# Interleaving the next group's LayerNorm and quantization with the scan of the current group, in a bidirectional state-space layer with a quantized gate

## The chip, the cores and the metric

The kernel runs on all 8 cores of one Trainium2 chip. Each core computes one sequence of the batch by itself; nothing is exchanged. The metric is the device time of the slowest core, in microseconds (us). It is given as the median of several executions. Engines are named as in the profile: PE is TensorE's matmul, PEld its weight load, DVE VectorE, ACT ScalarE, POOL GpSimd, SP SyncE. A "q" behind a name (POOLq) is the queue from which that engine issues DMAs.

## The reference, cut to what matters

Each core has `u` of 4096 x 1024. The layer is a residual around a product of a recurrent branch pair and a gate:

```
xn = layernorm(u)                                  # 1024 wide
zxbcdt = xn @ in_proj_w.T                          # z 2048, x 2048, B 64, C 64, dt 16
branch(zxbcdt, conv_w, dt_bias, A_log, D):
    dt = softplus(dt + dt_bias); A = -exp(A_log)
    x, B, C = split(silu(causal_conv4(xBC)))       # 16 heads of 128
    h_t = h_{t-1} * exp(dt_t*A) + dt_t * x_t B_t'  # state 64 per head
    y_t = h_t C_t + D*x_t
    yz = y * silu(z)
    return yz * rsqrt(mean(yz^2) + eps) * norm_w
s = (branch forward + branch on the reversed sequence, reversed back) @ out_proj_w.T
g = silu(mx_quantize(xn) @ mx_quantize(W).T + bias)   # blocks of 32, 6-bit grid
out = u + s * g
```

## The kernel before

The sequence is cut into 16 groups of `G` = 256 positions, each of two chunks of `Q` = 128. `pass_A` goes over the groups from the last to the first and runs the backward branch up to its scan; it stores the in-projection and the branch's output to HBM. `pass_B` goes forward over the groups: it loads both, computes the gate's two products (`z` and the quantized FFN product), the forward convolution and scan, then gating, norm, out-projection and residual.

Each engine has its own instruction stream, in program order, written out by one Python program that is run once per engine. Order between engines is kept by counting semaphores: `tp` counts PE, `ts` ACT, `tv` DVE, and `qs`, `qu`, `qx`, `qd`, `qo` and others count DMAs of one purpose. In `p.op`, a wait given as a pair such as `("tv", tvm)` is for a marked count; a wait given as a string such as `"ts"` is for the count of everything issued on that semaphore up to this place in the program. Waits are instructions of their own in the stream of the waiting engine, so whatever stands behind a waiting instruction waits too. Each DMA issue also waits for the DMA before it on the same semaphore.

A group of `pass_A` runs: in-projection (L914 to L924), convolution (`conv_dir`, DVE), transposes of its result to `Xtm` and `Btm` (SP), `dt_pipeline` (short operations of DVE and ACT, ending in six small DMAs `s_scr`, `sflat`, `b3c` on ACT's queue), then `pro` for the next group (L974), then `scan_chunk` for both chunks. A group of `pass_B` has the matmuls for `z` and the FFN first and four additions and two Silu for `gff` (L1262, L1272) behind `dt_pipeline`; then `pro` and the two `scan_chunk` again.

`pro` does, for each of the two 128-row tiles of the next group: load `u2` on GpSimd's queue, `ln_tile` (statistics on DVE, Ln and Exp on ACT at L361 and L365, the result `xn2` on DVE), a transposing DMA to `xnT`, and in `pass_B` also `quantize_tile` (two halves of some fifteen DVE operations, L1004 to L1086, ending in `xd2`) and a transposing DMA to `xdT`. Both tiles use the one buffer `u2`, so the second load waits for the first tile's DVE operations. The load's waits are `"tv"` and `"qo"`.

`scan_chunk` has a first part for each half `hq` of the heads: PE forms the decay sums in PSUM, ACT takes their Exp twice (`gq` at L687, `mtq` at L704; for `hq` 1 both lie in the tile `ur`), and DVE makes from them `bwq`, `diagq`, `gcq` and the final `mtq` (L709 to L746, the mark `opv` behind them). The second part, again for each half, is 32 small matmuls in two blocks of 16 (L777 to L787) with ACT's copies to `hT` (L790) and `convX` (L797). For `hq` 1 DVE makes a new `gcq` (L757) first. The first matmul of a chunk and the decay sums wait on `"ts"`, the Exp at L704 on `"tv"`:

```
            mm(ps[:, 3072:3072 + 128], v["convBC"][0:64, 0, csl],
               v["convBC"][0:64, 1, csl], True, True,
               wait=["ts", ("tv", tvm), "qd", "qy"])
...
                p.op("scalar",
                     lambda e, mtq_h=mtq_h, dsl=dsl: e.activation(
                         mtq_h, ps[:, dsl], AF.Exp),
                     wait=[("tp", t2v), "tv"], inc="ts")
```

Of the kernel before, what the change touches and what calls it, by code (L numbers as in the profile page):

```python
# [20 lines left out]
G = 256  # L21
NG = L // G
# [65 lines left out]
def make_program(debug=0):  # L88
# [133 lines left out]
    def prog(nc, p):  # L222
        shared = {}
# [3 lines left out]
        dr = state["dr"]  # L227
        sb = state["sb"]
# [13 lines left out]
        def ld(dst, src, wait=(), inc="qc", q="scalar"):  # L242
            p.op(q, lambda e: e.dma_start(out=dst, in_=src),
                 wait=wait, inc=inc, dma=True)
# [403 lines left out]
                         in_=dr["s_scr"][:, 3 + j_, :]),  # L648
                     inc="qd", dma=True)

        def scan_chunk(dirn, c, hTa, hTb, q_rot, tvm):
            anchor = (Q - 1) if dirn == "fw" else 0
            csl = slice(c * Q, (c + 1) * Q)
            v = sb
# [8 lines left out]
               wait=["ts", ("tv", tvm), "qd", "qy"])  # L663
            p.op("scalar",
                 lambda e: e.copy(v["cbt"][:], ps[:, 3072:3072 + 128]),
                 wait=["tp"], inc="ts")
            cbv = p.mark("ts")
            ph = []
            for hq in range(2):
# [11 lines left out]
                   wait=["qd", "ts", ("tv", tvm)])  # L681
# [7 lines left out]
                     wait=[("tp", t1v), "ts", ("tv", tvm)], inc="ts")  # L689
                gv = p.mark("ts")  # L690
                for nn in range(2):
# [4 lines left out]
                       wait=[("ts", gv)] if nn == 0 else ())  # L696
# [20 lines left out]
                     wait=[("ts", mtv), ("ts", cbv), "tv", "qo"],  # L717
                     inc="tv")
# [8 lines left out]
                     wait=["tv"], inc="tv")  # L727
                if hq == 0:
# [7 lines left out]
                         wait=["tv"], inc="tv")  # L736
# [7 lines left out]
                     wait=["tv"], inc="tv")  # L744
# [4 lines left out]
                     wait=["tv"], inc="tv")  # L749
                opv = p.mark("tv")  # L750
                ph.append((h0, pd, mtq_h, gq_h, bwq_h, diagq_h, opv))
            for hq in range(2):
                h0, pd, mtq_h, gq_h, bwq_h, diagq_h, opv = ph[hq]
                if hq == 1:
# [8 lines left out]
                         wait=[("tp", ymv0), "tv"], inc="tv")  # L763
                    opv = p.mark("tv")
                for half4 in range(2):
                    sev = p.mark("ts")
                    for hh4 in range(4):
# [7 lines left out]
                        elif hh4 == 0:  # L775
# [3 lines left out]
                           wait=w0)  # L779
# [14 lines left out]
                         wait=[("tp", smv)], inc="ts")  # L794
# [6 lines left out]
                     wait=[("tp", ymv)], inc="ts")  # L801
# [14 lines left out]
        def pass_A():  # L816
# [16 lines left out]
            for i in range(8):  # L833
                ld(sb["um"][:], dr["fwt"][i * 128:(i + 1) * 128, :],
                   wait=["tv"], inc="qw")
# [4 lines left out]
                qv = p.mark("tv")  # L840
                p.op("scalar",
                     lambda e, i=i: e.dma_start(
                         out=dr["wbfF"][i * 128:(i + 1) * 128, :],
                         in_=sb["xd2"][:, 0, :]),
                     wait=[("tv", qv)], inc="qw", dma=True)
                mk_st = p.mark("qw")
            shared["qfv"] = p.mark("qw")
            q_rot = [0, 0]
            rot = {"n": 0, "mk": [0, 0]}

            def pro(t0):
                for s_ in range(2):
                    ld(sb["u2"][:],
                       dr["u"][t0 + s_ * 128:t0 + (s_ + 1) * 128, :],
                       wait=["tv", "qo"], inc="qu", q="gpsimd")
                    ln_tile(s_, False)
                    xnv = p.mark("tv")
                    tpv = p.mark("tp")
                    p.op("sync",
                         lambda e, s_=s_, xnv=xnv, tpv=tpv: e.dma_start(  # L860
                             out=sb["xnT"][:, :, s_ * 128:(s_ + 1) * 128],
                             in_=sb["xn2"][:, s_, :].rearrange(
                                 "p (k f) -> p k f", k=8),
                             transpose=True),
                         wait=[("tv", xnv), ("tp", tpv), ("qs", wTv)],
                         inc="qs", dma=True)
                return p.mark("qs")

            prev = {"tv": p.mark("tv"), "ts": p.mark("ts"),
                    "tp": p.mark("tp")}  # L870
            xv = pro((NG - 1) * G)
            for gi in range(NG - 1, -1, -1):
                if gi == 2:
                    bbo = sb["warena"][:, 32768:40960].rearrange(
                        "p (t c) -> p t c", t=4)
                    for c0 in range(0, 8, 4):
# [18 lines left out]
                        out=sb["nwtile"][:],  # L895
                        in_=dr["normw"].rearrange("(k f) -> f k", f=128),
# [6 lines left out]
                                               transpose=True),  # L903
                         wait=[("qw", None)], inc="qs", dma=True)
# [23 lines left out]
                def halo_bw():  # L928
# [13 lines left out]
                         out=dr["sp_x"][gi],  # L942
# [31 lines left out]
                if gi > 0:  # L974
                    xv = pro((gi - 1) * G)
# [119 lines left out]
        def pass_B():  # L1095
# [26 lines left out]
            for half in range(2):  # L1122
# [23 lines left out]
            yzn_ap = sb["Xtm"][:].rearrange("p m q -> p (m q)").rearrange(  # L1146
                "p (i t) -> p i t", i=NH)

            def pro(t0):
                for s_ in range(2):  # L1150
                    ld(sb["u2"][:],
                       dr["u"][t0 + s_ * 128:t0 + (s_ + 1) * 128, :],
                       wait=["tv", "qo"], inc="qu", q="gpsimd")
                    ln_tile(s_, True)
                    xnv = p.mark("tv")
                    tpv = p.mark("tp")
                    p.op("sync",
                         lambda e, s_=s_, xnv=xnv, tpv=tpv: e.dma_start(
                             out=sb["xnT"][:, :, s_ * 128:(s_ + 1) * 128],
                             in_=sb["xn2"][:, s_, :].rearrange(  # L1160
                                 "p (k f) -> p k f", k=8),
                             transpose=True),
                         wait=[("tv", xnv), ("tp", tpv), ("qs", wdv)],
                         inc="qs", dma=True)
                    quantize_tile(sb["xd2"][:, s_, :], rst_is_one=False)
                    qv = p.mark("tv")
                    p.op("sync",
                         lambda e, s_=s_, qv=qv: e.dma_start(
                             out=sb["xdT"][:, :, s_ * 128:(s_ + 1) * 128],
                             in_=sb["xd2"][:, s_, :].rearrange(  # L1170
                                 "p (k f) -> p k f", k=8),
                             transpose=True),
                         wait=[("tv", qv)], inc="qs", dma=True)
                return p.mark("qs")

            prev = {"tv": p.mark("tv"), "ts": p.mark("ts"),
                    "tp": p.mark("tp")}
# [1 line left out]
            for gi in range(NG):  # L1179
# [95 lines left out]
                         wait=[("tv", gfv), "ts"], inc="ts")  # L1275
                ggv = p.mark("ts")
                tvm = p.mark("tv")
                if gi < NG - 1:
                    xv = pro(t0 + G)
                for c in range(CPG):  # L1280
                    p.op("tensor", lambda e: e.nop(),
                         wait=[("qs", trv), ("tv", tvm), "ts"])
                    scan_chunk("fw", c, sb["hT0"][:], sb["hT0"][:], q_rot,
                               tvm)
                yfv = p.mark("ts")
                opvs = [None, None]
                urvs = [None, None]
# [207 lines left out]
```

How the kernel before makes its waits and increments, by code:

```python
    def op(self, eng_name, fn, wait=(), inc=None, dma=False):  # L66
        if self.eng_name == eng_name:
            for w in wait:
                if isinstance(w, str):
                    s, v = w, self.cnt[w]
                else:
                    s, v = w
                    if v is None:
                        v = self.cnt[s]
                self.eng.wait_ge(self.h[s], v)
            if dma and inc is not None:
                self.eng.wait_ge(self.h[inc], self.cnt[inc])
            instr = fn(self.eng)
            if inc is not None:
                instr.then_inc(self.h[inc], 16 if dma else 1)
        if inc is not None:
            self.cnt[inc] += 16 if dma else 1
```

## Time and profile before

| | us |
|---|---|
| median of 3 runs (lowest, highest) | 7017.65 (7011.57, 7019.2) |
| the profiled execution, whole | 7007.59 |
| its span, core 0 (all cores 6983.4 to 7006.0) | 7006.0 |
| PE busy | 2635.8 (38%) |
| DVE busy | 2894.5 (41%) |
| ACT busy | 1314.3 (19%) |
| mean granted TensorE clock | 0.591 of 2.4 GHz |
| pass A's groups, from about 290 to 2950; pass B's from about 3020 to the end | |

Busy times are of one core. A row of the order of time gives the start, the duration, the engine, the line and the operation with its tiles, and in brackets how long the engine had been idle and what released it. Where a wait was for several semaphores, the one that came last by the profile is named. Merged rows carry a count (x2). All matmuls have the line of the helper `mm` (L239) and all loads by `ld` that of L243, so tiles tell them apart.

### The profile page before, as it was taken

How to read it: one execution, taken by the hardware profiler on the slowest of the kernel's cores; microseconds unless marked ns; L12 is line 12 of the kernel's file. 1: busy time of each engine (PE TensorE's matmuls, PEld its weight loads, DVE VectorE, ACT ScalarE, POOL GpSimd, SP SyncE). 2: the span in 40 equal slices, each digit the busy share in tenths (PEclk: the TensorE clock that was granted, in tenths of full speed). 3: DMA queues.
4: the chain of work that ended last, by engine and by line, in shares of the span. 5: the costliest groups of instructions: out<-in, count | busy, mean ns of one | idle time of the engine just before them, and what ended most of it. 6: DMA issues, size and time to landing. Idle time of an engine off the chain costs nothing.

```text
span 7006.0 us, 47131 instructions; the slowest of 8 cores (6983.4 to 7006.0 us)
## 1 busy us (share of the span) xinstructions
PE 2635.8 (38%) x12296; PEld 1268.2 (18%) x12296; DVE 2894.5 (41%) x5730; ACT 1314.3 (19%) x1939; POOL 125.4 (2%) x234
## 2 busy tenths in 40 slices
PE   0133444444433234315225334433522533443354
PEld 0011122222211112102112112111211211221121
DVE  2533333333443133353454354354345335435433
ACT  0021222222212112112111212211211221211112
POOL 0000000000000000000000000000000000000000
PEclk9955555555555555556566556556656655655665
DMA  4111110111111321121010011011101001110100
GB/s 91 40 33 34 35 29 29 29 29 35 35 29 35 88 58 35 44 60 32 19 42 26 22 41 34 26 27 37 31 19 42 26 22 41 35 33 20 41 28 19
DMA packets 364339, 250.45 MB, mean 36 GB/s; under 512 B 319456, under 2 KB 321761, under 8 KB 355890
## 3 DMA queue, kind: packets, MB, share of 16 engines
q0 software_dynamic: 30448, 132.95, 6.1%
q1 hardware_dynamic: 297216, 74.76, 5.4%
q10 hardware_dynamic: 36418, 39.72, 1.7%
q8 instruction: 110, 1.80, 0.1%
q14 instruction: 147, 1.20, 0.1%
HBM read 117.33 MB, written 68.19 MB: 26 GB/s over the span
## 4 chain that ended last, share of the span: by engine, by line
DVE 31%; PE 29%; DMA 14%; ACT 14%; issue 10%; DVEq 1%; ACTq 1%; POOLq 0%; POOL 0%; SPq 0%
PE ps L239 29%; DVE qv L424 6%; DVE convX L432 3%; DMA u<-u 2%; ACT convX L797 2%; DMA sflat<-s_scr 2%; DVE convX L404 2%; ACT convX L509 2%; DMA b3c<-s_scr 2%; DMA stgX<-sp_x 1%; ACT Xtm L1305 1%; DVE convX L410 1%; DVEq L75 1%; ACT hT L790 1%; DMA ybw<-sp_y 1%
## 5 line engine op out<-in xcount | busy, mean ns | idle before, releaser
L239 PE MATMUL ps<-convBC 64*128 64x128 bf16 x64 | 16.8, 262 | 2553.0 <-DVE um L371 1335.9
L239 PE MATMUL ps<-xnT,warena 128*128 128x256 bf16 (+2 forms) x4480 | 595.1, 294 | 457.6 <-DMA xnT<-xn 194.7
L239 PEld LDWEIGHTS ps<-xnT,warena 128*128 128x128 bf16 (+2 forms) x4480 | 441.6, 106 | 614.0 <-issue 524.2
L424 DVE TENSOR_TENSOR qv<-stgX,cwX 128x1012 bf16<-128x1012 bf16 x384 | 465.8, 1213 | 40.7 <-DVE convX L432 0.9
L239 PEld LDWEIGHTS ps<-convBC 64*128 64x128 bf16 x64 | 6.4, 100 | 2569.6 <-issue 2569.6
L239 PE MATMUL ps<-sflat,ones 3*64 3x512 bf16 (+1 forms) x512 | 282.7, 603 | 461.3 <-ACT mtq L704 244.6
L709 DVE TENSOR_TENSOR bwq<-Btm,mtq 128x512 bf16<-128x512 bf16 x64 | 44.3, 692 | 807.2 <-ACT mtq L704 807.2
L239 PE MATMUL ps<-warena,Xtm 128*128 128x512 bf16 x1024 | 293.5, 457 | 179.9 <-DVE u L1390 102.6
L790 ACT CAST hT<-ps 64x512 bf16<-64x512 f32 x256 | 148.2, 579 | 1019.7 <-PE ps L239 1019.7
L239 PE MATMUL ps<-gcq,hT 64*128 64x128 bf16 x1024 | 292.3, 285 | 0.0
L404 DVE TENSOR_SCALAR convX<-stgX,cwX,cbX 128x253 bf16<-128x253 bf16 x512 | 175.9, 343 | 273.5 <-ACT stgX L909 208.7
L432 DVE TENSOR_TENSOR convX<-convX,qv 128x1012 bf16<-128x1012 bf16 x384 | 264.6, 689 | 40.7 <-DVE qv L424 0.9
L509 ACT ACTIVATE convX<-convX 128x4096 bf16<-128x4096 bf16 x32 | 115.7, 3616 | 603.4 <-DVE convBC L503 603.3
L361 ACT ACTIVATE mv<-mv,epsb 128x1 f32<-128x1 f32 x64 | 18.8, 294 | 1022.5 <-DVE mv L357 762.8
L239 PE MATMUL ps<-ur,Xtm 128*128 128x128 bf16 x512 | 145.3, 284 | 162.7 <-ACT convX L797 110.2
L239 PE MATMUL ps<-mtq,Xtm 128*128 128x128 bf16 x512 | 145.0, 283 | 136.9 <-ACT ur L704 84.8
L757 DVE TENSOR_TENSOR gcq<-ur,convBC 64x1024 bf16<-64x1024 bf16 x64 | 43.7, 683 | 333.8 <-PE ps L239 333.8
L239 PEld LDWEIGHTS ps<-warena,Xtm 128*128 128x128 bf16 x1024 | 113.7, 113 | 352.4 <-issue 277.6
L353 DVE BATCH_NORM_STATS2 bns<-u 128x6 f32<-128x512 f32 x64 | 44.4, 694 | 318.3 <-DMA u<-u 318.3
L239 PE MATMUL ps<-Xtm,ones128b 128*1 128x128 bf16 x1024 | 95.5, 267 | 203.8 <-ACT Xtm L1305 203.8
L1338 DVE CAST rbc<-ps 128x256 bf16<-128x256 f32 x32 | 13.6, 424 | 383.8 <-PE ps L239 383.8
L239 PEld LDWEIGHTS ps<-sflat,ones 3*64 3x64 bf16 (+1 forms) x512 | 48.0, 116 | 666.8 <-issue 666.8
(164 smaller groups left out, 4845.3 us busy)
## 6 DMA issues: line engine op xcount, KB each, us to landing
u<-u POOLq DMA_DIRECT2D x64, 512.0 KB, 4.0
sp_x<-stgX POOLq DMA_DIRECT2D x16, 1024.0 KB, 4.2
sp_y<-convX POOLq DMA_DIRECT2D x16, 1024.0 KB, 4.8
stgX<-sp_x POOLq DMA_DIRECT2D x16, 1024.0 KB, 6.4
ybw<-sp_y POOLq DMA_DIRECT2D x16, 1024.0 KB, 5.0
ur<-u POOLq DMA_DIRECT2D x32, 512.0 KB, 4.0
out<-ostg ACTq DMA_DIRECT2D x32, 256.0 KB, 2.0
out<-u ACTq DMA_DIRECT2D x32, 256.0 KB, 2.5
```

Of the source, the lines that this page charges most:

```text
L75: self.eng.wait_ge(self.h[s], v)
L239: lambda e: e.matmul(out_ap, lhsT, rhs, start=start, stop=stop),
L353: p.op("vector", lambda e: e.bn_stats(sb["bns"][:, 0:6], uap[:, 0:512]), wait=["qu", "tv"], inc="tv")
L404: lambda e, i=i: e.tensor_scalar(cvX[:, i, osl0], stX[:, i, isl0], sb["cwX"][:, i, 0:1], sb["cbX"][:, i:i + 1], op0=ALU.mult, op1=ALU.add),
L410: lambda e, i=i: e.tensor_scalar(cvX[:, i, esl0], sb["haloX"][:, i, hsl0], sb["cwX"][:, i, 0:1], sb["cbX"][:, i:i + 1], op0=ALU.mult, op1= ...
L424: e.tensor_tensor(scr3, stX[:, t4, isl], sb["cwX"][:, t4, tap:tap + 1].broadcast_to([128, 4, n_main]), op=ALU.mult),
L432: e.tensor_tensor(cvX[:, t4, osl], cvX[:, t4, osl], scr3, op=ALU.add),
L509: lambda e: e.activation(cvX[:].rearrange("p i t -> p (i t)"), cvX[:].rearrange("p i t -> p (i t)"), AF.Silu),
L709: lambda e, bwq_h=bwq_h, mtq_h=mtq_h: e.tensor_tensor(bwq_h.rearrange("p (h n) -> p h n", h=8), v["Btm"][:, c, :].unsqueeze(1).broadcast_t ...
L790: lambda e, h0=h0, half4=half4: e.copy(hTb[:, (h0 + half4 * 4) * 128: (h0 + half4 * 4 + 4) * 128], ps[0:64, 3584:3584 + 512]),
L797: lambda e, h0=h0, pd=pd, csl=csl: e.copy(sb["ystg"][:, h0:h0 + 8, csl], ps[:, pd:pd + 1024].rearrange("p (h t) -> p h t", h=8)),
L1305: lambda e, buf=buf, tsl=tsl: e.activation(yzn_ap[:, :, tsl], sb[buf][:, :, tsl], AF.Square),
```

## The change

`pro` is cut into four pieces, `pa` and `pb` for each tile, in both passes. `pa` is the load and `ln_tile`; `pb` is the transposing DMA and, in `pass_B`, `quantize_tile` with its transposing DMA. `scan_chunk` gets an argument `fill_fn`, which is called right behind the Exp at L704, before DVE's `bwq`, and issues the next piece. The two chunks with two halves each take all four pieces in order: load and norm of tile 0, transpose (and quantization) of tile 0, the same two for tile 1. The operations themselves, and what each waits for by name, are unchanged; the counts that a string wait and a mark stand for are those at the new places. The first group of each pass still has its prologue in one block, and the last has none.

```diff
-        def scan_chunk(dirn, c, hTa, hTb, q_rot, tvm):
+        def scan_chunk(dirn, c, hTa, hTb, q_rot, tvm,
+                       fill_fn=None):
...
                 mtv = p.mark("ts")
+                if fill_fn is not None:
+                    fill_fn()
                 p.op("vector",
...
+            def pro_pieces(t0):
+                pieces = []
+                for s_ in range(2):
+                    def pa(s_=s_):
+                        ld(sb["u2"][:],
+                           dr["u"][t0 + s_ * 128:t0 + (s_ + 1) * 128, :],
+                           wait=["tv", "qo"], inc="qu", q="gpsimd")
+                        ln_tile(s_, True)
+
+                    def pb(s_=s_):
+                        xnv = p.mark("tv")
+                        tpv = p.mark("tp")
+                        p.op("sync",
+                             lambda e, s_=s_, xnv=xnv, tpv=tpv: e.dma_start(
+                                 out=sb["xnT"][:, :,
+                                              s_ * 128:(s_ + 1) * 128],
+                                 in_=sb["xn2"][:, s_, :].rearrange(
+                                     "p (k f) -> p k f", k=8),
+                                 transpose=True),
+                             wait=[("tv", xnv), ("tp", tpv), ("qs", wdv)],
+                             inc="qs", dma=True)
+                        quantize_tile(sb["xd2"][:, s_, :], rst_is_one=False)
+                        qv = p.mark("tv")
...
+                        shared["xvB"] = p.mark("qs")
+                    pieces.append(pa)
+                    pieces.append(pb)
+                return pieces
...
-                if gi < NG - 1:
-                    xv = pro(t0 + G)
+                fills = pro_pieces(t0 + G) if gi < NG - 1 else []
+
+                def ff(fills=fills):
+                    if fills:
+                        fills.pop(0)()
                 for c in range(CPG):
                     p.op("tensor", lambda e: e.nop(),
                          wait=[("qs", trv), ("tv", tvm), "ts"])
                     scan_chunk("fw", c, sb["hT0"][:], sb["hT0"][:], q_rot,
-                               tvm)
+                               tvm, fill_fn=ff)
+                while fills:
+                    fills.pop(0)()
+                if gi < NG - 1:
+                    xv = shared["xvB"]
```

`pass_A` is changed alike, with `ln_tile(s_, False)`, no quantization and `shared["xvA"]`. `pro` itself now calls the four pieces one after the other.

## Rows read from the trace of the kernel before

**Rows 1.** The page's first line.

```profile
span 7006.0 us, 47131 instructions; the slowest of 8 cores (6983.4 to 7006.0 us)
```

**Rows 2.** Waits of PE: who waited <- for whom, us in total, times, longest.

```profile
PE ps L239 <- DVE um L371: 1335.9, 15, 91.4
PE ps L239 <- ACT mv L365: 1013.9, 15, 68.3
```

**Rows 3.** Order of time, ACT, pass A, first and fifteenth group.

```profile
383.17 0.29 ACT L361 ACTIVATE mv<-mv,epsb 128x1 f32<-128x1 f32 x1 [17.52 <-DMA b3c<-s_scr]
383.55 0.20 ACT L365 ACTIVATE mv<-mv 128x1 f32<-128x1 f32 x1
...
393.67 0.27 ACT L665 CAST cbt<-ps 128x128 bf16<-128x128 f32 x1 [1.00 <-PE ps L239]
...
2707.82 0.29 ACT L361 ACTIVATE mv<-mv,epsb 128x1 f32<-128x1 f32 x1 [17.29 <-DMA b3c<-s_scr]
...
2718.58 0.27 ACT L665 CAST cbt<-ps 128x128 bf16<-128x128 f32 x1 [1.03 <-PE ps L239]
```

**Rows 4.** The same, group 0 of pass A, with no prologue behind it.

```profile
2873.45 3.49 ACTq L646 DMA_DIRECT2D b3c<-s_scr  x3
2878.77 0.27 ACT L665 CAST cbt<-ps 128x128 bf16<-128x128 f32 x1 [28.68 <-PE ps L239]
```

**Rows 5.** The same, pass B, first and fifteenth group.

```profile
3136.28 2.20 ACT L1272 ACTIVATE gff<-gff 128x1024 bf16<-128x1024 bf16 x2
...
3246.41 1.00 ACT L797 CAST convX<-ps 128x1024 bf16<-128x1024 f32 x1
...
6625.01 2.20 ACT L1272 ACTIVATE gff<-gff 128x1024 bf16<-128x1024 bf16 x2
...
6735.23 1.00 ACT L797 CAST convX<-ps 128x1024 bf16<-128x1024 f32 x1
```

**Rows 6.** The same, last group of pass B, with no prologue behind it.

```profile
6874.43 2.20 ACT L1272 ACTIVATE gff<-gff 128x1024 bf16<-128x1024 bf16 x2
...
6879.45 1.28 ACT L687 ACT_TABLE_LOAD   x1 [1.47 <-PE ps L239]
...
6948.00 1.00 ACT L797 CAST convX<-ps 128x1024 bf16<-128x1024 f32 x1
...
6956.02 0.36 ACT L1318 ACTIVATE rrow<-ps,epsb 1x128 bf16<-1x128 f32 x1 [2.16 <-PE ps L239]
```

**Rows 7.** The same, group 7 of pass B.

```profile
4928.93 1.02 ACT L704 ACTIVATE mtq<-ps 128x1024 bf16<-128x1024 f32 x1 [13.63 <-DVE xd L1086]
```

**Rows 8.** Order of time, DVE, group 7 of pass B.

```profile
4884.92 0.75 DVE L376 TENSOR_SCALAR xn<-um,mv 128x1024 bf16<-128x1024 f32 x1 [5.24 <-ACT mv L365]
4885.77 0.69 DVE L1004 TENSOR_REDUCE qsc<-um 128x16 f32<-128x512 f32 x1
...
4901.32 0.69 DVE L1086 TENSOR_TENSOR xd<-qv,qsc 128x512 bf16<-128x512 f32 x1 [0.17 <-DVE qsc L1082]
...
4930.26 0.69 DVE L709 TENSOR_TENSOR bwq<-Btm,mtq 128x512 bf16<-128x512 bf16 x1 [1.43 <-ACT mtq L704]
...
4933.43 0.69 DVE L746 TENSOR_TENSOR mtq<-mtq,ddiag 128x1024 bf16<-128x1024 bf16 x1
...
4945.66 0.68 DVE L757 TENSOR_TENSOR gcq<-ur,convBC 64x1024 bf16<-64x1024 bf16 x1 [5.25 <-PE ps L239]
```

**Rows 9.** DMA issues: tiles, queue, count, KB each, median us to landing.

```profile
u<-u POOLq DMA_DIRECT2D x64, 512.0 KB, 4.0
...
xnT<-xn SPq DMA_TRANSPOSE x64, 2.7
```

**Rows 10.** Order of time, PE, group 7 of pass B, first chunk's outputs.

```profile
4937.18 0.26 PE L239 MATMUL ps<-mtq,Xtm 128*128 128x128 bf16 x1 [1.32 <-ACT ur L704]
...
4947.21 0.27 PE L239 MATMUL ps<-ur,Xtm 128*128 128x128 bf16 x1 [1.72 <-ACT convX L797]
```

**Rows 11.** Stages: busy us and instructions by engine, clock, DMA share, GB/s.

```profile
4957.00:4993.00 36.00, 23.84 (x81) 8.99 (x81) 7.12 (x11) 8.58 (x12) 0.00 (x0) 0.50 0.00 1
```

More of the change, by code:

```diff
@@ L849, in pass_A @@
             rot = {"n": 0, "mk": [0, 0]}
-            def pro(t0):
[L852 to L867, printed above, removed]
+            def pro_pieces(t0):
[5 more added lines that the diff above has]
+                           wait=["tv", "qo"], inc="qu", q="gpsimd")
+                        ln_tile(s_, False)
+                    def pb(s_=s_):
[8 more added lines that the diff above has]
+                                 transpose=True),
+                             wait=[("tv", xnv), ("tp", tpv), ("qs", wTv)],
+                             inc="qs", dma=True)
+                        shared["xvA"] = p.mark("qs")
+                    pieces.append(pa)
+                    pieces.append(pb)
+                return pieces
+            def pro(t0):
+                for f in pro_pieces(t0):
+                    f()
+                return shared["xvA"]
             prev = {"tv": p.mark("tv"), "ts": p.mark("ts"),
@@ L973, in pass_A @@
                 tvm = p.mark("tv")
-                if gi > 0:
-                    xv = pro((gi - 1) * G)
+                fills = pro_pieces((gi - 1) * G) if gi > 0 else []
+                def ff(fills=fills):
+                    if fills:
+                        fills.pop(0)()
                 for c in range(CPG - 1, -1, -1):
@@ L1147, in pass_B @@
                 "p (i t) -> p i t", i=NH)
-            def pro(t0):
[L1150 to L1174, printed above, removed]
@@ new lines, in pro_pieces, with pa, pb @@
+            def pro_pieces(t0):
+                pieces = []
+                for s_ in range(2):
+                    def pa(s_=s_):
+                        ld(sb["u2"][:],
+                           dr["u"][t0 + s_ * 128:t0 + (s_ + 1) * 128, :],
+                           wait=["tv", "qo"], inc="qu", q="gpsimd")
+                        ln_tile(s_, True)
+                    def pb(s_=s_):
+                        xnv = p.mark("tv")
+                        tpv = p.mark("tp")
+                        p.op("sync",
+                             lambda e, s_=s_, xnv=xnv, tpv=tpv: e.dma_start(
+                                 out=sb["xnT"][:, :,
+                                              s_ * 128:(s_ + 1) * 128],
+                                 in_=sb["xn2"][:, s_, :].rearrange(
+                                     "p (k f) -> p k f", k=8),
+                                 transpose=True),
+                             wait=[("tv", xnv), ("tp", tpv), ("qs", wdv)],
+                             inc="qs", dma=True)
+                        quantize_tile(sb["xd2"][:, s_, :], rst_is_one=False)
+                        qv = p.mark("tv")
+                        p.op("sync",
+                             lambda e, s_=s_, qv=qv: e.dma_start(
+                                 out=sb["xdT"][:, :,
+                                              s_ * 128:(s_ + 1) * 128],
+                                 in_=sb["xd2"][:, s_, :].rearrange(
+                                     "p (k f) -> p k f", k=8),
+                                 transpose=True),
+                             wait=[("tv", qv)], inc="qs", dma=True)
+                        shared["xvB"] = p.mark("qs")
+                    pieces.append(pa)
+                    pieces.append(pb)
+                return pieces
@@ L1176, in pass_B @@
+            def pro(t0):
+                for f in pro_pieces(t0):
+                    f()
+                return shared["xvB"]
             prev = {"tv": p.mark("tv"), "ts": p.mark("ts"),
@@ L1283, in pass_B @@
                     scan_chunk("fw", c, sb["hT0"][:], sb["hT0"][:], q_rot,
-                               tvm)
+                               tvm, fill_fn=ff)
+                while fills:
+                    fills.pop(0)()
+                if gi < NG - 1:
+                    xv = shared["xvB"]
                 yfv = p.mark("ts")
```

5 lines of the change are left out of this document (added).

## The prediction

> **What bounds the kernel now.** Three views were read in this order. First the list of what TensorE (PE) waited for. Its two longest lines are waits in front of the scan, 1335.9 us in 15 groups of pass B, put down to the `um` operation, and 1013.9 us in 15 groups of pass A, put down to the Exp of `ln_tile` [rows 2]. Both belong to the prologue `pro` of the next group. So the question is what lies at the end of these waits. No engine is full; the kernel is one chain of PE, VectorE (DVE), ScalarE (ACT) and DMAs in which each stage waits for the one before.
>
> Then the order of time on ACT around the scan of pass A. After the last `b3c` DMA, ACT goes straight on to the Ln of the first tile, and the scan's first copy `cbt` comes 10.50 us after that Ln in the first group and 10.76 in the fifteenth (393.67 - 383.17, 2718.58 - 2707.82; the mean of the 15 is 10.67) [rows 3]. Group 0 has no prologue behind it. There `cbt` comes 2878.77 - 2876.94 = 1.83 us after the third `b3c` issue has ended [rows 4]. What fills the difference is the second tile: its load waits for the first tile's last DVE operation, because both use `u2`, and only when it has landed and has been normalised is the ACT count reached on which `scan_chunk`'s first matmul waits (`"ts"`, the count at that place of the program).
>
> Last, the same for pass B. From the end S of the second Silu at L1272 to the end of the scan's last copy it takes 3247.41 - 3138.48 = 108.93 us in the first group and 6736.23 - 6627.21 = 109.02 in the fifteenth, mean 108.9 [rows 5]. In the last group, which has no prologue, it takes 6949.00 - 6876.63 = 72.37 us [rows 6]. So the prologue costs 36.5 us a group here. It is on the path because the Exp at L704 waits for everything on DVE, both `quantize_tile` calls included: in group 7 it starts at 4928.93 after a 13.63 us wait for `xd` [rows 7].
>
> **What the change does, by parts.** The same instructions are issued, in four pieces per group instead of one block. A piece follows the Exp at L704 of each half `hq` of each chunk. Call the end of the hq 0 Exp M.
>
> *The front of the scan.* No prologue operation stands ahead of the first matmul any more. In pass A the gain is 10.67 - 1.83 = 8.8 us a group (third `b3c` DMA to first matmul as in group 0). In pass B S to the end becomes the 72.37 us of the last group plus what the pieces add inside the scan.
>
> *Piece 1 and piece 3 (load, `ln_tile`) at hq 0.* ACT does Ln and Exp behind the L704 Exp: 0.08 + 0.38 + 0.20 = 0.66 us [rows 3]. PE's matmuls for hq 1 wait on the ACT count, so they move by 0.7. That is on the path, twice a group: 1.4 us. The statistics of the first tile wait for nothing new (load released by the end of `dt_pipeline` or the `gff` adds, as before). On DVE `xn` starts about 0.9 after M and has a slot of 0.85 (4885.77 - 4884.92), then the five operations of hq 0 take 3.86 (4934.12 - 4930.26) [rows 8]: done at M + 5.6. In the scan as it is they end at M + 4.2 (M = 4929.95). The hq 1 Exp, which waits for them, starts at about M + 6.1 without the 0.7 (PE's outputs follow it at 4937.18 = M + 7.2, and it lasts 1.02 [rows 7, 10]) and at M + 6.75 with it, so this delay is covered with 1.1 us to spare. If that cover were gone it would cost the excess, tenths per chunk.
>
> *The second load.* It is queued on GpSimd behind nothing of the scan but the DVE count of the chunk before. In pass A this is about M + 16.4, as in the row of `gcq` (4945.66, 15.7 after M) [rows 8] plus 0.7. A load lands in a median of 4.0 us [rows 9], the two statistics and the aggregate take under 2.5, and the next hq 0 Exp ends 36 us after M. So some 12 us are spare (two equal chunks share about 71 of the 72.37 us, 35.4 each). Behind this load on GpSimd's queue stand only the `sp_y` store (pass A) and the `ur` load (pass B), both after the scan. The 4 to 6 us of this load and its statistics, which stood on the path, vanish into the first chunk.
>
> *Pieces 2 and 4 (transpose; in pass B also `quantize_tile`) at hq 1.* In pass A only a transpose on SyncE's queue. It now waits for matmuls of hq 1, lands in 2.7 us [rows 9], and the second one is out some 17 us before the scan ends. Nobody needs it before the next in-projection: nothing. What is queued behind it on SyncE is the next group's `Xtm` transpose, far later.
> In pass B one quantization takes 16.24 us of DVE (4885.77 to 4902.01 over two halves) [rows 8], ahead of hq 1's DVE work. It starts at M + 5.7 and ends at M + 21.95. It waits for no transpose: `xnT` is issued near M + 6.6 and lands before the first `xd` write near M + 13. Then four operations at a spacing of 0.79 (3.1), `gcq` (0.8) and 0.3 to PE: the hq 1 outputs start at M + 26.2. Without the pieces they start at 4947.21 - 4929.95 = M + 17.3 [rows 7, 10]. PE's hq 0 outputs and ACT's copies run meanwhile and are what hides the rest. This is 8.9 us a chunk, 17.8 a group; it holds the 0.7 of piece 1. The quantized tile's transpose, of the same size as `xnT`'s, ends inside the scan. The load of the second tile is released at M + 25.9, lands by M + 32 (I allow 6 us, half as much again as the median), and is normalised by M + 35, while the next M is 35.4 + 8.9 = 44.3 away: 9 us spare.
>
> *The activation table.* The load of 1.28 us in front of the Ln after Silu moves to the scan's first Exp, as in the last group (6879.45) [rows 6]. It is in the 72.37. The number of loads stays.
>
> **The sum.** Pass B: 108.9 - (72.4 + 17.8) = 18.7 us a group, times 15 = 280. Pass A: 8.8 - 1.4 = 7.4, times 15 = 111. Together 391. The profiled execution took 7007.59 (span 7006.0 [rows 1]); 7007.6 - 391 = 6617. The median of the runs shown lies 10 us, 0.14%, above the profiled one, so the forecast for the median is 6625, 5.6% less.
> Bounds of what the trace doesn't show, the DVE work inside the scan: below, it can't cost less than nothing, which would give 7007.6 - 15 x 36.5 - 15 x 8.8 = 6328, but DVE has only the gaps of each chunk, and the instruction order puts 16 us into one of them; above, that none of the quantization overlaps (first rival). I take the value from the order of instructions, which is nearest to the rows.
> TensorE's clock gives and takes nothing here: in the scan it is granted 0.50, 1.2 GHz, as it is [rows 11], so the new pauses cannot lower it, and the stages behind the scan start from the same state.
>
> **Rivals.**
> (a) *The quantization is not hidden by the hq 0 outputs.* If the first output matmuls also waited for piece 2, they would start after M + 22 and hq 1's about 10.0 later (4947.21 - 4937.18) [rows 10], at M + 32.3: 6.1 us more a chunk, 183 in all, 6810. For it: many waits here take "the count so far" of an engine. Against it: the mark `opv` that these matmuls wait for is taken before the piece is issued.
> (b) *Ln between two Exps costs table loads.* Two loads per `ln_tile`, four a group, 30 groups, by the row of 1.28 us [rows 6]: 154 us, 6780. Against it: in the last group the table was loaded for an Exp, and a Ln at 6956.02 followed with no load between [rows 6]. The Trainium skill ("ScalarE: Activation LUTs", Table sets: the hidden batching unit) says the same, that one set holds both exp and ln. Its section What ACT_TABLE_LOAD costs gives about 2.66 us for a switch, drain included; by that this rival would be 30 x 4 x 2.66 = 319 us, 6945. Where page and row differ I go by the row.
> (c) *Slower: the second tile's load comes late.* It is now between the chunks, on DVE and ACT ahead of the scan's own work of the second chunk, so a late load stops everything. It has 9 to 12 us to spare, and a group saves 7.4 or 18.7, so it would decide the sign only if the load took some 22 to 34 us instead of 4 to 6. At 40 us each, pass A would lose about 15 a group and pass B 6: 7330. Against it: the load is alone in its queue, and its wait ends in chunk one.
> (d) *No change*: the waits only move. This needs DVE's whole prologue to stay on the path in both passes; the second load alone contradicts it.
>
> **How the numbers follow.** Forecast 0.86, with a range of its own from 6585 to 6665 (1.3 us a group either way). Rival (a) 0.05, (b) 0.03, (c) 0.02, (d) 0.01, and 0.03 for a mixture that keeps part of the gain. The range 6565 to 6685 leaves out the rivals and a little of the forecast's tails. Faster by over 0.2% (about what a measurement of this kernel can tell from no change) is everything but (c) and (d) and a part of the mixture: 0.96; within it 0.015; slower 0.025.
>
> **What would show it.** PE's two long waits give way to one for `b3c` (pass A) and one for the second `gff` Silu (pass B). In pass A `cbt` stands about 2 us behind the last `b3c` issue, and the scan is 1.4 us longer than in group 0. In pass B S to the end of the scan is 90 us, with a PE gap of about 9 us ahead of each hq 1 output block, put down to `gcq` or DVE. The first load of a group stays where it is, the second lands inside the first chunk's last third (pass A) or between the chunks (pass B). 15 table loads move from L361 to L687. The prediction is wrong if the hq 0 outputs wait for `xd`, if `bns` waits for `u` in the second chunk with PE idle, or if DVE's operations beside PE and DMA traffic take longer than these rows.

## The result and the profile after

The changed kernel takes 6632.96 us in the median of 8 runs (6627.3 to 6635.53), against 7013.83 us (7008.1 to 7022.59) for the kernel before in the same comparison: a ratio of 0.9454, 95% interval 0.9444 to 0.9464, or 381 us less. A second comparison on another chip gave 0.9468 (0.9452 to 0.9484). The forecast was 6625 us, with a range from 6565 to 6685.

The page of the profile after, its span and the busy times:

```profile
span 6627.3 us, 47131 instructions; the slowest of 8 cores (6602.0 to 6627.3 us)
...
PE 2633.1 (40%) x12296; PEld 1267.4 (19%) x12296; DVE 2893.6 (44%) x5730; ACT 1315.4 (20%) x1939; POOL 125.2 (2%) x234
```

All busy times are those of before to within 3 us. The same work stands closer together.

What PE waited for, in the changed kernel (engine, releaser, us in total, times, longest):

```profile
PE ps L239 <- ACT gff L1309: 981.2, 16, 63.8
PE ps L239 <- DMA b3c<-s_scr: 955.3, 16, 71.5
PE ps L239 <- DVE gcq L760: 307.5, 30, 10.5
...
PE ps L239 <- ACT mv L365: 127.4, 60, 2.4
```

The `um` line of [rows 2] is gone, and the line of `mv` has fallen from 1013.9 us to 127.4. In their place stand the waits that the prediction named: the second `gff` Silu in pass B, 981.2 us in 16 groups where the `um` line had 1335.9 in 15, and the last `b3c` DMA in pass A. These are now the length of the stages ahead of the scan. Inside the scan two lines are to be read. The 30 waits for `gcq`, 307.5 us or 10.25 each, are new. The 60 for the Exp of `ln_tile` (`mv`) last 2.1 us each; they stand where PE waited for the Exp at L704 before, for 1.4 us wherever DVE didn't hold that Exp up.

ACT in order of time, pass A, the first and the fifteenth group, which answers to [rows 3]:

```profile
376.50 3.69 ACTq L646 DMA_DIRECT2D b3c<-s_scr  x3
381.94 0.27 ACT L666 CAST cbt<-ps 128x128 bf16<-128x128 f32 x1 [19.53 <-PE ps L239]
...
389.68 0.29 ACT L361 ACTIVATE mv<-mv,epsb 128x1 f32<-128x1 f32 x1
390.06 0.20 ACT L365 ACTIVATE mv<-mv 128x1 f32<-128x1 f32 x1
...
2597.61 3.46 ACTq L646 DMA_DIRECT2D b3c<-s_scr  x3
2602.88 0.27 ACT L666 CAST cbt<-ps 128x128 bf16<-128x128 f32 x1 [18.75 <-PE ps L239]
```

The third `b3c` issue ends at 380.19, and `cbt` comes 1.75 us later, as in group 0 [rows 4]. Ln and Exp now stand in the scan, right behind the chunk's first Exp at L705 (L704 before). Over the 15 groups the distance from the last `b3c` issue to `cbt` fell from 10.8 to 1.9 us and the scan grew from 70.06 to 71.36.

The same for pass B, which answers to [rows 5]:

```profile
3026.60 2.21 ACT L1309 ACTIVATE gff<-gff 128x1024 bf16<-128x1024 bf16 x2
...
3118.43 1.01 ACT L800 CAST convX<-ps 128x1024 bf16<-128x1024 f32 x1
...
6265.79 2.21 ACT L1309 ACTIVATE gff<-gff 128x1024 bf16<-128x1024 bf16 x2
...
6357.58 1.01 ACT L800 CAST convX<-ps 128x1024 bf16<-128x1024 f32 x1
```

From the end of the second Silu to the end of the scan it takes 3119.44 - 3028.81 = 90.63 us in the first group and 6358.59 - 6268.00 = 90.59 in the fifteenth, in the mean of the 15 90.79. It was 108.92. The last group, which has no pieces, has 72.2 as before.

One group of pass B (the ninth), its first chunk on ACT:

```profile
4887.09 1.28 ACT L688 ACT_TABLE_LOAD   x1 [1.47 <-PE ps L239]
4888.38 1.02 ACT L688 ACTIVATE gq<-ps 64x1024 bf16<-64x1024 f32 x1
4892.97 1.02 ACT L705 ACTIVATE mtq<-ps 128x1024 bf16<-128x1024 f32 x1 [3.57 <-PE ps L239]
4894.08 0.30 ACT L361 ACTIVATE mv<-mv,epsb 128x1 f32<-128x1 f32 x1
```

The table load has moved from the Ln to the first Exp, and the Ln behind the Exp at L705 needs none. M, the end of that Exp, is 4893.99. On DVE (`qsc` at L1027 is the first operation of a quantization, `xd` its last):

```profile
4894.92 0.75 DVE L376 TENSOR_SCALAR xn<-um,mv 128x1024 bf16<-128x1024 f32 x1 [13.67 <-ACT mv L365]
4895.84 0.69 DVE L712 TENSOR_TENSOR bwq<-Btm,mtq 128x512 bf16<-128x512 bf16 x1 [0.17 <-DVE xn L376]
...
4899.01 0.69 DVE L749 TENSOR_TENSOR mtq<-mtq,ddiag 128x1024 bf16<-128x1024 bf16 x1
4899.81 0.69 DVE L1027 TENSOR_REDUCE qsc<-um 128x16 f32<-128x512 f32 x1
...
4903.51 0.29 DVE L1079 TENSOR_SCALAR qm<-qau 128x512 bf16<-128x512 bf16 x1
4904.26 0.29 DVE L1083 TENSOR_SCALAR qm<-qau 128x512 bf16<-128x512 bf16 x1 [0.46 <-DVE qm L1079]
...
4915.70 0.69 DVE L1109 TENSOR_TENSOR xd<-qv,qsc 128x512 bf16<-128x512 f32 x1 [0.17 <-DVE qsc L1105]
4916.57 0.69 DVE L712 TENSOR_TENSOR ostg<-Btm,ur 128x512 bf16<-128x512 bf16 x1 [0.17 <-DVE xd L1109]
...
4919.74 0.68 DVE L760 TENSOR_TENSOR gcq<-ur,convBC 64x1024 bf16<-64x1024 bf16 x1
4925.00 0.69 DVE L353 BATCH_NORM_STATS2 bns<-u 128x6 f32<-128x512 f32 x1 [4.58 <-DMA u<-u]
...
4926.91 0.75 DVE L371 TENSOR_SCALAR um<-u,mv 128x1024 f32<-128x1024 f32 x1
```

And on PE, the first output block of hq 0 and those of hq 1 of both chunks:

```profile
4901.91 0.26 PE L239 MATMUL ps<-mtq,Xtm 128*128 128x128 bf16 x1 [1.32 <-ACT ur L705]
...
4920.68 0.26 PE L239 MATMUL ps<-ur,Xtm 128*128 128x128 bf16 x1 [10.49 <-DVE gcq L760]
...
4965.23 0.26 PE L239 MATMUL ps<-ur,Xtm 128*128 128x128 bf16 x1 [10.13 <-DVE gcq L760]
```

The queue of DVE is to be read against M. `xn` starts at M + 0.9, `bwq` at M + 1.9, and the hq 0 work ends at M + 5.7. The quantization fills M + 5.8 to M + 22.4, `gcq` of hq 1 ends at M + 26.4, and PE starts the hq 1 outputs at M + 26.7 after 10.49 us of waiting. The hq 0 outputs started at M + 7.9, straight behind ACT's Exp and not behind `xd`: some 7 us of the quantization are hidden there. The second tile is loaded and `um` written by M + 33.7; the next Exp ends 44.9 after M.

The second chunk as a stage (busy us of PE, PEld, DVE, ACT, POOL, the granted clock, DMA share, GB/s), beside [rows 11]:

```profile
4931.00:4976.00 45.00, 23.79 (x81) 8.97 (x81) 21.43 (x42) 8.98 (x13) 0.00 (x0) 0.50 0.05 12
```

It takes 9 us more than before for the same PE work, DVE is busy 21.43 us instead of 7.12, and the clock stays at 0.50.

### The profile page after: what moved, and what is told of

Its sections match the earlier page's. It is cut to its first block, busy times and chain, and to the rows that moved or that the text cites. A ratio compares the mean times of both kernels' runs of the same rounds, so it can differ in the third digit from the quotient of the medians.

```text
span 6627.3 us, 47131 instructions; the slowest of 8 cores (6602.0 to 6627.3 us)
## 1 busy us (share of the span) xinstructions
PE 2633.1 (40%) x12296; PEld 1267.4 (19%) x12296; DVE 2893.6 (44%) x5730; ACT 1315.4 (20%) x1939; POOL 125.2 (2%) x234
## 4 chain that ended last, share of the span: by engine, by line
DVE 35%; PE 26%; DMA 14%; ACT 13%; issue 10%; DVEq 1%; ACTq 1%; POOLq 0%; POOL 0%; SPq 0%
PE ps L239 26%; DVE qv L424 7%; DVE convX L432 3%; DMA b3c<-s_scr 2%; DMA sflat<-s_scr 2%; DVE convX L404 2%; ACT convX L509 2%; ACT convX L800 2%; DVEq L75 1%; ACT Xtm L1349 1%; DMA stgX<-sp_x 1%; DVE convX L410 1%; DMA ybw<-sp_y 1%; DVE qv L468 1%; ACT mtq L705 1%
## 5 line engine op out<-in xcount | busy, mean ns | idle before, releaser
L239 PE MATMUL ps<-convBC 64*128 64x128 bf16 x64 | 16.8, 262 | 2008.3 <-ACT gff L1309 981.2
L239 PE MATMUL ps<-sflat,ones 3*64 3x512 bf16 (+1 forms) x512 | 282.9, 603 | 368.9 <-ACT mv L365 127.4
L239 PE MATMUL ps<-ur,Xtm 128*128 128x128 bf16 x512 | 144.0, 281 | 418.9 <-DVE gcq L760 307.5
L382 DVE TENSOR_SCALAR xn<-u,mv 128x1024 bf16<-128x1024 f32 x32 | 26.0, 812 | 419.9 <-ACT mv L365 419.9
L239 PE MATMUL ps<-mtq,Xtm 128*128 128x128 bf16 x512 | 144.0, 281 | 137.3 <-ACT ur L705 83.8
L376 DVE TENSOR_SCALAR xn<-um,mv 128x1024 bf16<-128x1024 f32 x32 | 24.1, 753 | 393.8 <-ACT mv L365 393.5
L239 PE MATMUL ps<-Xtm,bwq 128*64 128x128 bf16 x512 | 160.3, 313 | 0.0
L239 PE MATMUL ps<-Xtm,ostg 128*64 128x128 bf16 x512 | 160.3, 313 | 0.0
```

The costliest lines, as they stand in the source:

```text
L239: lambda e: e.matmul(out_ap, lhsT, rhs, start=start, stop=stop),
```

## The experiments

All ratios are to the kernel before, run beside it on the same chip. Three chips were used, and on them that kernel had medians of 7022.6, 7020.5 and 7017.3 us. Expectations are on a scale on which it has 7014 and the change 6633, so differences to the kernel before are compared, not times. Each such difference is known to about 10 us. Where a time per group is given, it is the mean of the 15 groups with a prologue in that run's trace. Line numbers shift by a few from one kernel to the next.

### Each pass alone

The pieces in pass A only, and in pass B only:

```diff
-                fills = pro_pieces(t0 + G) if gi < NG - 1 else []
+                fills = []
+                if gi < NG - 1:
+                    pro(t0 + G)
```

```diff
-                fills = pro_pieces((gi - 1) * G) if gi > 0 else []
+                fills = []
+                if gi > 0:
+                    pro((gi - 1) * G)
```

> The pieces in pass A alone; pass B keeps its prologue in one block. Theory (each group of pass A loses the 9.0 us in front of its scan and pays 1.3 us inside it, 15 groups): 115 us in the groups, of which the trace of the change kept 112, so 7014 - 113 = 6901 us. Rival (the two passes help each other, or part of the 381 us comes from somewhere else than the 30 prologues): this run and its counterpart do not add up to 381 us, by more than 10.

> The pieces in pass B alone. Theory (108.9 us from the second gff Silu to the end of the scan become 90.9, 15 groups): 7014 - 268 = 6746 us. Rival as for the counterpart: the two gains do not add up to 381 us.

Measured: pass A alone 6917.28 us, ratio 0.9849 (0.9834 to 0.9863), 105 us less. Pass B alone 6757.08 us, 0.9621 (0.9607 to 0.9636), 266 us less. Together 371, against 381 and 374 for the whole change in its two comparisons: the two gains add up to within what can be told. The gain comes from the 30 prologues, with no sign of another source. Pass A gave 8 us less than expected, which is within what a difference is known to. In its trace the distance and the scan changed as in the whole change (1.9 and 71.3 us), but its period per group fell by 7.2 us and not by 7.7, since the six small DMAs of `dt_pipeline` took 10.1 us a group there against 9.7 before. This is not shown to come from the change: with the pieces in pass B only, whose pass A is that of before, they took 10.3.

### The quantization in halves, and behind `gcq`

The first half of the columns stays where the change has the whole, and the second half is a third piece, `pc`, behind the hq 1 `gcq`. In pass A the third piece is empty.

```diff
-                        quantize_tile(sb["xd2"][:, s_, :], rst_is_one=False)
+                        quantize_tile(sb["xd2"][:, s_, :], rst_is_one=False,
+                                      halves=(0,))
+
+                    def pc(s_=s_):
+                        quantize_tile(sb["xd2"][:, s_, :], rst_is_one=False,
+                                      halves=(1,))
...
```

and behind the hq 1 `gcq` in `scan_chunk`:

```diff
                         wait=[("tp", ymv0), "tv"], inc="tv")
                     opv = p.mark("tv")
+                    if fill_fn is not None:
+                        fill_fn()
```

> The change, with each quantization cut in two: the first half of the columns stays between the hq 0 and hq 1 work of DVE, the second half goes behind the hq 1 gcq. Theory (what is left on the path in pass B is the part of a piece that is longer than the time that PE needs for the hq 0 outputs; half a quantization, 8.2 us, fits): hq 1 outputs start at M + 18 instead of M + 26.5 in each chunk, 8.4 us x 2 x 15 = 252 us less, 6381 us. Rival (any DVE work there delays the chunk by its length, and the second half delays the next chunk or the gating by its own): the sum of DVE work is the same, so 6633 us again, within 30.

Measured: 6395.5 us, ratio 0.9105 (0.909 to 0.9121), 627 us less than before and 246 less than the change. PE in a group of pass B, first outputs of hq 0 and hq 1:

```profile
4778.11 0.27 PE L239 MATMUL ps<-mtq,Xtm 128*128 128x128 bf16 x1 [1.32 <-ACT ur L705]
...
4788.74 0.27 PE L239 MATMUL ps<-ur,Xtm 128*128 128x128 bf16 x1 [2.36 <-DVE gcq L760]
```

DVE beside it (end of the first half, `gcq`, end of the second half):

```profile
4783.76 0.69 DVE L1113 TENSOR_TENSOR xd<-qv,qsc 128x512 bf16<-128x512 f32 x1 [0.17 <-DVE qsc L1109]
...
4787.80 0.68 DVE L760 TENSOR_TENSOR gcq<-ur,convBC 64x1024 bf16<-64x1024 bf16 x1
...
4795.95 0.69 DVE L1113 TENSOR_TENSOR xd<-qv,qsc 128x512 bf16<-128x512 f32 x1 [0.17 <-DVE qsc L1109]
```

M is 4770.18 here. The hq 1 outputs start at M + 18.6, after 2.36 us of waiting, and the second half ends at M + 26.5, before the next chunk needs DVE. The distance from the second Silu to the scan's end is 74.3 us, against 90.8. The same DVE operations in another order cost 16.5 us a group less. The rival, that the sum of DVE work decides, has fallen.

Then the whole quantization behind `gcq`: piece `pc` with both halves, none at hq 1.

> The change, with each whole quantization behind the hq 1 gcq of its chunk instead of between the hq 0 and hq 1 work of DVE. Theory: the hq 1 outputs no longer wait (8.9 us less a chunk), but in the first chunk the load of the second tile is released 7 us later than now and its statistics come about 4 us after the Exp that they follow, and in the second chunk DVE ends 5 us after the scan, which the gating waits for: 18 - 4 - 5.5 = 8 to 9 us a group less, 6633 - 130 = 6500 us, between 6480 and 6530. Rival (where the quantization stands does not matter as long as it is inside the scan): 6633 us, within 20.

Measured: 6547.09 us, ratio 0.9319 (0.9304 to 0.9335), 473 us less than before and 92 less than the change. The direction is the theory's, the size fell short of the least that was expected by about 10 us. DVE in a group (statistics of the second tile, last quantization of the second tile, first operation of the gating):

```profile
4898.28 0.69 DVE L353 BATCH_NORM_STATS2 bns<-u 128x6 f32<-128x512 f32 x1 [5.63 <-DMA u<-u]
...
4933.23 0.69 DVE L1113 TENSOR_TENSOR xd<-qv,qsc 128x512 bf16<-128x512 f32 x1 [0.17 <-DVE qsc L1109]
4934.02 1.23 DVE L1344 TENSOR_TENSOR convX<-convX,siluz 128x2048 bf16<-128x2048 bf16 x1
```

The two costs are there: the statistics come at 4898.28 with DVE idle for 5.63 us before, so the second chunk starts late, and the gating starts 0.1 us behind the last `xd`. The scan's last copy ended about 6 us earlier. From the Silu to the end of the scan the groups take 78.5 us, 12.3 less than in the change. The gating begins 5.8 us behind the scan in the mean where it began 0.2 behind it in the change, so 6.7 us a group are left, times 15 = 100; measured were 92. Of the three terms expected, the 18 us were the one that was off: the hq 1 outputs start 8.5 us earlier in each chunk, 17.0 in all, since the 0.7 us of Ln and Exp stay on the path. The late statistics cost 4.6 us where 4 were expected, and the gating 5.6 where 5.5 were.

### The quantization at hq 0

```diff
                 mtv = p.mark("ts")
-                if fill_fn is not None:
+                if fill_fn is not None and hq == 0:
+                    fill_fn()
                     fill_fn()
```

> The change, with transpose and quantization issued with the load and norm of their tile, at hq 0, ahead of DVE's hq 0 work: nothing is left for PE to do meanwhile but the decay sums of hq 1. Theory (7 us of each quantization are hidden by the hq 0 outputs and no more): hq 1 outputs at M + 33.5 instead of M + 26.5, 7 us x 2 x 15 = 210 us more, 6843 us. In pass A only the transpose moves: nothing. Rival (the quantization is not hidden by the hq 0 outputs at all, as one of the rivals of the prediction has it): no change against 6633 us.

Measured: 6855.73 us, ratio 0.9762 (0.9748 to 0.9777), 165 us less than before and 216 more than the change. Now PE waits ahead of the hq 0 outputs:

```profile
PE ps L239 <- ACT ur L705: 551.0, 64, 17.1
```

In the change this line had 83.8 us in 63 times. The Exp of hq 1 waits for all of DVE's hq 0 work, and the hq 0 outputs wait for that Exp, so with the quantization ahead of it PE has nothing to do. This measures what the hq 0 outputs hide in the change: 216 / 30 = 7.2 us a chunk.

### Load and norm ahead of the second Exp

The place of pieces 1 and 3 is moved ahead of the Exp at L705; pieces 2 and 4 stay.

```diff
                 t2v = p.mark("tp")
+                if fill_fn is not None and hq == 0:
+                    fill_fn()
                 p.op("scalar",
...
                 mtv = p.mark("ts")
-                if fill_fn is not None:
+                if fill_fn is not None and hq == 1:
                     fill_fn()
```

> The change, with load and norm (pieces 1 and 3) issued ahead of the second Exp of hq 0 instead of behind it; the quantization stays whole, at hq 1. Theory: pass A gains 1.3 us a group, the whole of what the pieces cost there; pass B gains 1.5 us a chunk, since DVE does xn ahead of M and its hq 0 work ends at M + 4.2 instead of M + 5.7, and DVE sets the start of the hq 1 outputs: 20 + 45 us, 6633 - 65 = 6568 us. Rival (only ACT's 0.66 us count, DVE's xn is hidden): 60 x 0.66 = 40 us, 6593 us.

Measured: 6573.14 us, ratio 0.936 (0.9346 to 0.9374), 447 us less than before and 66 less than the change. The scan of pass A takes 69.96 us again (71.36 in the change, 70.06 before), and from the Silu to the scan's end it takes 87.8 in pass B: 3.0 less. With 15 groups each that is 21 + 45 = 66 us, as measured. The rival's 40 is not what the groups show.

Both edits together:

> As the run with the halves, and load and norm of a tile (pieces 1 and 3) issued ahead of the second Exp of hq 0 instead of behind it, so that ACT does Ln and Exp while PE forms the decay sums. Theory (the 0.66 us of Ln and Exp lie on the path only because PE's hq 1 sums wait for ACT's count behind them; ACT is idle for 3.6 us ahead of the second Exp): pass A gains 1.3 us a group, pass B the 0.8 us a chunk that the halves leave: 20 + 24 us less than the halves, 6337 us. Rival (ACT's time is hidden wherever it stands, and the 1.3 us of pass A come from DVE): same as the halves, 6381 us.

Measured: 6347.35 us, ratio 0.9038 (0.9024 to 0.9051), 675 us less than before and 294 less than the change. ACT in the first chunk of a group of pass B:

```profile
4733.39 0.30 ACT L361 ACTIVATE mv<-mv,epsb 128x1 f32<-128x1 f32 x1
4733.77 0.20 ACT L365 ACTIVATE mv<-mv 128x1 f32<-128x1 f32 x1
4736.86 1.02 ACT L707 ACTIVATE mtq<-ps 128x1024 bf16<-128x1024 f32 x1 [2.88 <-PE ps L239]
```

Ln and Exp stand in the pause in which PE forms the decay sums; the second Exp still waits 2.88 us for PE behind them. From the Silu to the scan's end it takes 72.4 us, and the scan of pass A 69.9: the times of the groups that have no prologue at all (72.4 in [rows 6], and 70.0 in group 0 of pass A before). Inside these stretches the prologue is free in this version, and it is the fastest of those run here.

### The second load made longer

The second tile's load of each group three times, and six times, in a row, in both passes. `pro` calls the same pieces, so the opening prologue of each pass, which stands in one block with nothing beside it, gets the additional loads too:

```diff
-                        ld(sb["u2"][:],
-                           dr["u"][t0 + s_ * 128:t0 + (s_ + 1) * 128, :],
-                           wait=["tv", "qo"], inc="qu", q="gpsimd")
+                        for _ in range(3 if s_ == 1 else 1):
+                            ld(sb["u2"][:],
+                               dr["u"][t0 + s_ * 128:t0 + (s_ + 1) * 128, :],
+                               wait=["tv", "qo"], inc="qu", q="gpsimd")
```

> The change, with the second tile's load of each group issued three times in a row (same data, same buffer), each behind the landing of the one before; the statistics wait for the last. Theory (the load and its statistics have about 12 us to spare in both passes; two more loads take 8 to 9): 6633 us, within 15. Rival (a late load stops the second chunk at once): 8.5 us x 30 groups = 255 us more, 6888 us.

Measured: 6665.12 us, ratio 0.9491 (0.9477 to 0.9505), 355 us less than before, 26 more than the change in its first comparison and 19 more than in its second. That is more than the expected 15. The statistics do come late, and DVE idles 14 us for them:

```profile
4963.88 0.69 DVE L353 BATCH_NORM_STATS2 bns<-u 128x6 f32<-128x512 f32 x1 [14.01 <-DMA u<-u]
```

But nobody waits for it in the scans: from the Silu to the scan's end it is 90.86 us (90.79 in the change), the scan of pass A 71.45 (71.36), and ACT's Ln waited for the statistics only 4 times in all, as in the change, for the tiles of the two opening prologues:

```profile
ACT mv L361 <- DVE mv L357: 279.4, 4, 182.0
```

In the change these four waits took 263.3 us, 16.1 less. There lies what the run lost: in the opening prologues the two additional loads stand on the path. This is the Ln of the second tile in that of pass B, in the change, with three loads and with six:

```profile
2939.22 0.30 ACT L361 ACTIVATE mv<-mv,epsb 128x1 f32<-128x1 f32 x1 [25.28 <-DVE mv L357]
...
2965.68 0.29 ACT L361 ACTIVATE mv<-mv,epsb 128x1 f32<-128x1 f32 x1 [35.05 <-DVE mv L357]
...
3095.63 0.29 ACT L361 ACTIVATE mv<-mv,epsb 128x1 f32<-128x1 f32 x1 [46.37 <-DVE mv L357]
```

From the first tile's Ln to the second's it takes 25.9, 35.6 and 47.0 us there, and 9.0, 17.6 and 29.5 in the opening prologue of pass A. With three loads that is 9.8 + 8.6 = 18.3 us more in the whole kernel, and 19 to 26 were measured. The expectation counted only the groups in which the load is beside a scan.

> As the run with three loads, with six: five more than the change has. Theory (the second load costs nothing until its statistics pass the Ln behind the second chunk's Exp, and from there on every us of it is on the path): with three loads 4.7 us were left in pass A and some 2.5 in pass B; three more at 4.1 and 4.8 us go over by 7.6 and 11.9 us a group, 292 us over the run with three loads, or about 6950 us on the scale on which the change has 6633. Rival (later loads are hidden behind something else, or the extra traffic alone made the run with three loads longer): the same small step again, about 25 to 40 us, 6700 us.

Measured: 6929.87 us, ratio 0.9874 (0.9859 to 0.9888), 87 us less than before and 287 more than the change beside it. Now the Ln waits in every group:

```profile
ACT mv L361 <- DVE mv L357: 552.9, 34, 182.7
```

The scan of pass A takes 79.1 us, 7.7 more than in the change, as expected (7.6); pass B's distance is 99.6, 8.8 more, where 11.9 were expected: the five loads took 21.1 us together in the opening prologue of pass B, 4.2 each and not 4.8, and 12.4 were to spare. That makes 15 x 16.5 = 248 of the 287. The two opening prologues are 20.5 + 21.1 = 41.6 longer, which is the rest. The cost of a late load has an edge, and beyond it every us counts.

### The changed kernel again

> The changed kernel on the chip of this call, to see how far its ratio to the kernel before moves from chip to chip: 0.945 to 0.947.

Measured: 6643.21 us, ratio 0.9468 (0.9452 to 0.9484), where 0.9454 was measured first. The two intervals overlap.

## Why the prediction was right, point by point

**What bounded the kernel**: the two waits were what the change shortened, and both single-pass runs add up to the whole. Shown. The last rival, no change, has fallen with it.

**The front of the scan**: 8.8 us a group was forecast for pass A, 8.95 measured (10.82 to 1.87). The forecast took its 10.67 from the start of the Ln and its 1.83 from the end of the third `b3c` issue, 0.15 apart. In pass B the scan begins 1.0 us behind the Silu, as in the last group.

**Ln and Exp on the path**: 1.4 us a group was forecast for pass A, 1.3 measured; moving them away gave it back. DVE's delay of 1.5 us at hq 0 was covered in pass A. In pass B the prediction counted it within the 8.9 us of a chunk, rightly: there DVE sets the pace, and moving the norm gave back 1.5 us a chunk and not the 0.66 of ACT.

**The quantization inside the scan**: 8.9 us a chunk was forecast; the chunks of the trace grew by 9.2 us (44.76 from Exp to Exp instead of 35.55). The term was 0.3 us too small. The wait for `gcq` is longer than the forecast's gap of about 9 us, 10.25, because it replaces one of 1.72 that was there [rows 10]; with the 0.7 of Ln and Exp, 10.25 - 1.72 + 0.7 is again 9.2. In the group shown, 0.34 of it is a pause between two small operations (4903.51 to 4904.26, where 0.40 is the usual step), which the second chunk of the same group does not have: there the outputs start at M + 26.35 against the forecast 26.2. What causes it wasn't tested. That the hq 0 outputs run beside the quantization, against the first rival, is shown by their start at M + 7.9 and by the 216 us of the run that takes this cover away.

**The activation table**: the second rival has fallen. The load is before the scan's first Exp in every group of pass B, 16 in all, and the Ln between two Exps has none. The Trainium skill ("ScalarE: Activation LUTs", Table sets: the hidden batching unit) has both functions in one set, and the trace agrees. Of its figure of about 2.66 us a switch, drain included (What ACT_TABLE_LOAD costs), the rows show the load alone: it takes 1.28 us and the Exp starts 0.01 us behind its end (4887.09 + 1.28 = 4888.37, 4888.38). ACT was idle ahead of this load, which could hide a drain; where ACT is busy up to the load, as in `dt_pipeline` of the changed kernel, there is no room for one:

```profile
3004.82 0.42 ACT L529 ACTIVATE sp<-dt_t 16x256 f32<-16x256 f32 x1 [1.24 <-DVE dt_t L523]
3005.32 1.28 ACT L532 ACT_TABLE_LOAD   x1
3006.61 0.42 ACT L532 ACTIVATE sp<-sp 16x256 f32<-16x256 f32 x1
```

From the end of the one operation to the start of the next it takes 1.37 us.

**The second load**: it has about 13 us to spare in pass A and 12 in pass B (the forecast had 12 and 9). The rival that would have made the kernel slower has fallen; but the mechanism that it names exists, and its edge lies between the 9 us of lateness of the run with three loads and the 21 of the run with six.

**TensorE's clock**: it is 0.50, the level of 1.2 GHz, in the scans of all 32 groups before and after, with a pause of 10 us in each chunk of pass B now. PE's busy time in the whole kernel fell by 2.7 us only, so the clock gave and took nothing elsewhere either.

**The sum**: pass B gave 18.1 us a group and pass A 7.65 inside these stretches, 272 + 115 = 387 us, where 280 + 111 = 391 was forecast. The two misses have opposite signs, 8 us too much for pass B and 4 too little for pass A, so that the sum came out closer than its terms is in part luck. The spans differ by 378.7. The rest, 8 us, lies outside the scans. The six small DMAs of `dt_pipeline` took 10.0 us a group in pass A instead of 9.7, 22.4 instead of 19.5 in its last group, and 0.1 more in a group of pass B, 8.6 us together. As they also took 10.3 in a kernel whose pass A is that of before, this may be a difference between executions and no cost of the change; which it is was not tested.

## What to carry to other kernels

Work that is moved into the shadow of another engine is hidden only where its place in its own queue says so: the same 16 us of DVE cost nothing (in halves, with the norm ahead of the second Exp), 9 us or 16 us a chunk, depending on which operations with waiting readers stood behind them. Before placing a filler, write down for the host engine when each of its operations is really needed, and cut the filler to the gaps: here each half of 8 us fitted a gap in which the whole did not fit. A filler's short operations on a second engine (Ln and Exp here) count too if the critical engine waits for that engine's running count; put them ahead of an operation that is waiting anyway. And when an experiment changes a helper, look for every place that calls it: here the opening prologues explain what the two runs with additional loads lost outside the scans.

## What the runs showed of the hardware

A switch of the activation table cost 1.28 us and nothing behind it (1.29 us from the start of the load to the start of the next operation), and nothing ahead of it where ACT was busy (1.37 us from one operation to the next). The scan, granted 0.50 of the clock before, stayed there when PE's busy share in its second chunk went from 66 to 53% and DVE's from 20 to 48%. A load of 512 KB that was issued behind the landing of another one cost 4.1 to 4.9 us where it stood on the path (the opening prologues of the runs with three and six loads), and nothing inside the scan up to 9 us of lateness.
